# Scaling the last expert's tiles on ScalarE in every batch, with the order of the instructions written anew

## What is computed

```python
xn = layernorm(x)                                  # no scale or shift
q, k, v = xn @ Wq.T, xn @ Wk.T, xn @ Wv.T
attn = (q @ k.T) * tril(ones)                      # masked scores are 0, not minus infinity
attn = softmax(attn / sqrt(512)) @ v
gates = softmax(xn @ Wg); keep the top 2, divide by their sum
ffn = sum over experts e of gate[e] * (xn @ We[e] + be[e])
out = x + attn + ffn
```

## Time and profile before

| what | value |
|---|---|
| three runs, us | 120.26, 120.28, 120.30 (median 120.28) |
| profiled execution | 120.22 us, of which the span (first to last instruction) is 118.5 us |
| TensorE clock granted | full in the whole span |
| busy share of the span | TensorE 95%, VectorE 90%, ScalarE 84%, GpSimd 77% |

### The profile page before, as it was taken

How to read it: one execution, slowest core, us unless ns; L and a number is a source line. 1 busy time by engine, 2 the same in 40 slices (tenths; PEclk the granted TensorE clock), 3 DMA queues, 4 the chain that set the end, 5 groups by cost and what they waited for, 6 DMA issues and landing times.

```text
span 118.5 us, 2933 instructions
## 1 busy us (share of the span) xinstructions
PE 112.7 (95%) x733; PEld 103.5 (87%) x733; DVE 106.4 (90%) x532; ACT 99.0 (84%) x338; POOL 91.3 (77%) x183
## 2 busy tenths in 40 slices
PE   4986999999999999999999999999999999999990
PEld 4965879998999989998899989999899989899990
DVE  0689999989999899999999899999999898998892
ACT  2456899899897999899997989899997989978930
POOL 7349569899768996699768995799868995896970
PEclk9999999999999999999999999999999999999999
DMA  3759500000300011000300020000300030000033
GB/s 95 255 165 304 157 3 6 0 3 3 89 0 3 0 55 39 0 0 3 94 3 0 0 68 20 6 0 3 94 0 0 0 90 4 0 3 0 6 91 89
DMA packets 9233, 5.18 MB, mean 44 GB/s; under 512 B 384, under 2 KB 9088, under 8 KB 9216
## 3 DMA queue, kind: packets, MB, share of 16 engines
q1 hardware_dynamic: 8656, 4.66, 13.6%
q10 hardware_dynamic: 560, 0.33, 1.0%
HBM read 2.89 MB, written 2.10 MB: 42 GB/s over the span
## 4 chain that ended last, share of the span: by engine, by line
PE 87%; DMA 4%; ACT 3%; DVE 2%; SPq 1%; issue 1%; DVEq 0%
PE ring L248 15%; PE ring L252 14%; PE ring L249 14%; PE attb L306 13%; PE score L293 8%; PE score L252 4%; PE score L249 4%; PE score L248 4%; DMA w_f<-in_w_stacked_dram 4%; PE ring L324 3%; PE ring L345 2%; PE attb L358 1%; PE ring L335 1%; PE ring L337 1%; PE ring L334 1%; ACT c_s L906 1%
## 5 line engine op out<-in xcount | busy, mean ns | idle before, releaser
L922 ACT ACTIVATE ysc<-ring,gate 128x128 f32<-128x128 f32 x124 | 35.6, 388 | 0.8 <-PE ring L252 0.6
L248 PE MATMUL ring<-w_hi,xT_hi 128*128 128x512 f32 (+2 forms) x96 | 35.5, 370 | 0.4 <-ACT xT_hi L1001 0.4
L249 PE MATMUL ring<-w_lo,xT_hi 128*128 128x512 f32 (+2 forms) x96 | 32.5, 339 | 0.0
L252 PE MATMUL ring<-w_hi,xT_lo 128*128 128x512 f32 (+2 forms) x96 | 32.5, 338 | 0.0
L1130 POOL TENSOR_TENSOR ysc<-ysc,mix 128x256 f32<-128x256 f32 x31 | 22.9, 738 | 6.2 <-DVE mix L576 3.6
L1127 POOL TENSOR_TENSOR ysc<-ysc 128x256 f32<-128x256 f32 x31 | 22.8, 736 | 6.0 <-ACT ysc L922 6.0
L576 DVE SCALAR_TENSOR_TENSOR mix<-ring,gate,mix 128x128 f32<-128x128 f32 x65 | 22.4, 347 | 0.9 <-PE ring L252 0.3
L306 PE MATMUL attb<-c_s,probT 128*128 128x128 f32 x152 | 21.8, 274 | 0.0
L306 PEld LDWEIGHTS attb<-c_s,probT 128*128 128x128 f32 x152 | 20.1, 191 | 0.2
L248 PEld LDWEIGHTS ring<-w_hi,xT_hi 128*128 128x128 f32 x96 | 18.1, 189 | 2.1 <-ACT xT_hi L1001 0.6
L252 PEld LDWEIGHTS ring<-w_hi,xT_lo 128*128 128x128 f32 x96 | 18.1, 188 | 1.5 <-DVE xT_lo L509 0.2
(11 more groups left out here) (115 smaller groups left out, 237.8 us busy)
## 6 DMA issues: line engine op xcount, KB each, us to landing
x_all<-in_x_dram SPq DMA_DIRECT2D x7, 256.0 KB, 3.9
out_dram<-o_s SPq DMA_DIRECT2D x7, 256.0 KB, 2.3
w_f<-in_w_stacked_dram SPq DMA_DIRECT2D x1, 256.0 KB, 4.5
w_f<-in_w_stacked_dram SPq DMA_DIRECT2D x1, 192.0 KB, 4.4
w_f<-in_w_stacked_dram SPq DMA_DIRECT2D x1, 132.0 KB, 3.7
x_all<-in_x_dram ACTq DMA_DIRECT2D x1, 128.0 KB, 2.7
x_all<-in_x_dram SPq DMA_DIRECT2D x1, 128.0 KB, 2.5
wqk_s<-in_w_attention_dram ACTq DMA_DIRECT2D x1, 128.0 KB, 3.9
```

The lines of the kernel that those rows point to most:

```text
L248: nc.tensor.matmul(dst, hi, w_h, start=True, stop=False)
L249: nc.tensor.matmul(dst, hi, w_l, start=False, stop=False)
L252: return nc.tensor.matmul(dst, lo, w_h, start=False, stop=True)
L922: last = nc.scalar.mul(ysc[:, t, e, :], bank(f"A{t}", b)[:, e * P:(e + 1) * P], gate[:, b % 2, t, e:e + 1])
```

## The change

- ScalarE scales the last expert's product in every batch, four instructions of 128x128 (three in the last batch), behind `scale_experts(n, 0)`. `scale_last` and GpSimd's calls of it are gone.
- mix has five places per tile. B's results go to 0, 1 and 3 (`MIX_AT`), the scaled last expert to 2 in even and to 4 in odd batches, and GpSimd adds the pair 2:4 or 3:5. ScalarE therefore waits for the sums of two batches before, not of the one before.
- The order is written anew on all four engines, in the start, the loop and the end, and the ring's lists with it. In the start ScalarE makes w_hi of B first and of A later, GpSimd takes the bias split first, then w_lo of B, then of A; VectorE does the statistics of batch 1 before the second half of x_lo; TensorE takes the value sums behind two score tiles; ScalarE copies x of batch 1 before the first probabilities.

The diff, with eight columns of indentation taken off and the end's lists on TensorE and VectorE cut:

```diff
--- before.py
+++ after.py
@@ -52,12 +52,14 @@
 Y_AT, G_AT = P, 2 * P
 
 
-FIRST_GROUPS = """C0@0 C1@0 U@0 C2@0 C3@0 SV@0 B0@0 A0@0 X@1 A1@0 B1@0 U@1 C0@1 A2@0 C1@1 C2@1""".split()
-GROUPS = "B2- C3 A3- B3- SV DT- B0 A0 X+ A1 B1 U+ C0+ C1+ A2 C2+".split()
-LAST_GROUPS = """B2@-2 C3@-1 A3@-2 B3@-2 A0@-1 B0@-1 DT@-2 B1@-1 B2@-1 A1@-1 A2@-1 B3@-1 SV@-1 DT@-1 A3@-1""".split()
+FIRST_GROUPS = """C0@0 C1@0 U@0 C2@0 C3@0 SV@0 A0@0 X@1 B0@0 C0@1 A1@0 B1@0 U@1 A2@0 C1@1 C2@1""".split()
+GROUPS = "B2- C3 A3- B3- SV DT- B0 A0 X+ A1 C0+ B1 U+ C1+ A2 C2+".split()
+LAST_GROUPS = """B2@-2 C3@-1 A3@-2 B3@-2 A0@-1 B0@-1 DT@-2 B1@-1 B2@-1 A1@-1 SV@-1 B3@-1 A2@-1 A3@-1 DT@-1""".split()
 
 ROWS = 32
 G_ROW = 3
+
+MIX_AT = (0, 1, 3)
 
 
 class Chain:
@@ -136,7 +138,7 @@
 gsum, grec = (sb(n, [P, NT]) for n in ("gsum", "grec"))
 
 ysc = sb("ysc", [P, NT, 4, P])
-mix = sb("mix", [P, NT, 4, P])
+mix = sb("mix", [P, NT, 5, P])
 ffn = sb("ffn", [P, 2, NT, P])
 
 lhs_rows = sb("lhs_rows", [P, NT * ROWS], F32R)
@@ -396,24 +398,24 @@
     project_u(0)
     wide(0, "C", 2)
     wide(0, "C", 3)
-    value_sums(0)
     scores(0, 0)
     scores(0, 1)
-    wide(0, "B", 0)
+    value_sums(0)
+    wide(0, "A", 0)
     scores(0, 2)
-    wide(0, "A", 0)
     transpose_x(1)
     transpose_probs(0, 0)
+    wide(0, "B", 0)
+    scores(0, 3)
+    wide(1, "C", 0)
     wide(0, "A", 1)
-    transpose_probs(0, 1)
-    scores(0, 3)
     wide(0, "B", 1)
     project_u(1)
-    wide(1, "C", 0)
     wide(0, "A", 2)
-    attend(0, 0)
     wide(1, "C", 1)
     wide(1, "C", 2)
+    attend(0, 0)
+    transpose_probs(0, 1)
 
     for n in range(1, B - 1):
         wide(n - 1, "B", 2)
@@ -422,60 +424,60 @@
         scores(n, 0)
         transpose_probs(n - 1, 2)
         wide(n - 1, "A", 3)
+        wide(n - 1, "B", 3)
         transpose_probs(n - 1, 3)
-        wide(n - 1, "B", 3)
-        attend(n - 1, 2)
         value_sums(n)
         scores(n, 1)
+        attend(n - 1, 2)
         transpose_rows(n - 1)
         attend(n - 1, 3)
         bias(n - 1)
+        transpose_probs(n, 0)
         wide(n, "B", 0)
         wide(n, "A", 0)
         scores(n, 2)
-        transpose_probs(n, 0)
         transpose_x(n + 1)
         wide(n, "A", 1)
+        scores(n, 3)
+        transpose_probs(n, 1)
+        wide(n + 1, "C", 0)
         wide(n, "B", 1)
-        scores(n, 3)
         project_u(n + 1)
-        wide(n + 1, "C", 0)
         attend(n, 0)
-        transpose_probs(n, 1)
         wide(n + 1, "C", 1)
         wide(n, "A", 2)
         wide(n + 1, "C", 2)
 
...
@@ -572,8 +574,8 @@
         if i == 0 and with_y7:
 
             dve.wait_ge(S["x7_ready"], 1)
-        before = mix[:, t, i - 1, :] if i else mix[:, t, 3, :] if with_y7 else tile_ap(b, t)
-        ins = nc.vector.scalar_tensor_tensor(mix[:, t, i, :], bank(f"B{t}", b)[:, i * P:(i + 1) * P],
+        before = mix[:, t, i - 1, :] if i else mix[:, t, 4, :] if with_y7 else tile_ap(b, t)
+        ins = nc.vector.scalar_tensor_tensor(mix[:, t, MIX_AT[i], :], bank(f"B{t}", b)[:, i * P:(i + 1) * P],
                                              gate[:, b % 2, t, 4 + i:5 + i], before, ALU.mult, ALU.add)
         if i < 2:
             cnt["mix", b, t, i] = chain.mark(ins)
@@ -590,7 +592,7 @@
             chain.need(cnt["mix_a", e - 1])
         ins = nc.vector.scalar_tensor_tensor(
             mix[:, t, e % 2, :], bank(f"A{t}", b)[:, e * P:(e + 1) * P], gate[:, b % 2, t, e:e + 1],
-            mix[:, t, 2 if e == 0 else 1 - e % 2, :], ALU.mult, ALU.add)
+            mix[:, t, MIX_AT[2] if e == 0 else 1 - e % 2, :], ALU.mult, ALU.add)
         if e < 3:
             cnt["mix_a", e] = chain.mark(ins)
         else:
@@ -740,143 +742,143 @@
     a_low(0)
     x_lo_half(0, 0)
     first_sums(0)
-    x_lo_half(0, 1)
     normal_stats(1, 0)
-    token_sums_pairs(0)
     normal_stats(1, 1)
     normal_stats(1, 2)
     normal_stats(1, 3)
+    x_lo_half(0, 1)
+    token_sums_pairs(0)
     normal_finish(1)
     token_sums_later(0)
     u_lo(0)
     gate_max(0)
+    mask_scores(0, 0)
     gate_drop(0)
-    mask_scores(0, 0)
+    gate_below(0)
     mask_scores(0, 1)
-    gate_below(0)
     negate_max(0, 0)
+    gate_sum(0)
     negate_max(0, 1)
+    gate_rec(0)
     sv_rows(0, 0)
+    gate_out(0)
     sv_rows(0, 1)
-    gate_sum(0)
     sv_rows(0, 2)
-    gate_rec(0)
-    gate_out(0)
+    x_lo(1)
     mix_b(0, 0, 0)
+    token_sums(1)
     mix_b(0, 0, 1)
     mix_b(0, 0, 2)
-    x_lo(1)
-    token_sums(1)
 
     for n in range(1, B - 1):
+        mask_scores(n - 1, 2)
         mix_b(n - 1, 1, 0)
-        mask_scores(n - 1, 2)
         mix_b(n - 1, 1, 1)
         negate_max(n - 1, 2)
         mix_b(n - 1, 1, 2)
         u_lo(n)
         normal_stats(n + 1, 0)
         normal_stats(n + 1, 1)
-        normal_stats(n + 1, 2)
         mask_scores(n - 1, 3)
         mix_b(n - 1, 2, 0)
+        negate_max(n - 1, 3)
         mix_b(n - 1, 2, 1)
-        negate_max(n - 1, 3)
+        normal_stats(n + 1, 2)
         mix_b(n - 1, 2, 2)
+        token_sums_pairs(n)
+        mask_scores(n, 0)
         gate_max(n)
         normal_stats(n + 1, 3)
+        softmax_sum(n - 1)
+        token_sums_later(n)
+        softmax_tot(n - 1)
         gate_drop(n)
-        softmax_sum(n - 1)
-        token_sums_pairs(n)
-        softmax_tot(n - 1)
-        token_sums_later(n)
+        normal_finish(n + 1)
         gate_below(n)
-        normal_finish(n + 1)
+        negate_max(n, 0)
+        mask_scores(n, 1)
+        softmax_rec(n - 1)
+        negate_max(n, 1)
         mix_b(n - 1, 3, 0)
-        mask_scores(n, 0)
+        gate_sum(n)
         mix_b(n - 1, 3, 1)
-        gate_sum(n)
-        negate_max(n, 0)
+        gate_rec(n)
         mix_b(n - 1, 3, 2)
-        gate_rec(n)
-        softmax_rec(n - 1)
         gate_out(n)
-        mask_scores(n, 1)
         sv_rows(n, 0)
         sv_rows(n, 1)
+        sv_rows(n, 2)
         mix_b(n, 0, 0)
-        sv_rows(n, 2)
+        finish_tile(n - 1, 0)
+        finish_tile(n - 1, 1)
         mix_b(n, 0, 1)
-        finish_tile(n - 1, 0)
+        finish_tile(n - 1, 2)
         mix_b(n, 0, 2)
-        finish_tile(n - 1, 1)
-        negate_max(n, 1)
-        finish_tile(n - 1, 2)
-        finish_tile(n - 1, 3)
         x_lo(n + 1)
         token_sums(n + 1)
-
+        finish_tile(n - 1, 3)
+
...
+    sv_rows(B - 1, 0)
+    softmax_rec(B - 1)
+    sv_rows(B - 1, 1)
+    mix_b(B - 1, 3, 0)
     finish_tile(B - 2, 2)
-    mix_b(B - 1, 3, 0)
+    mix_b(B - 1, 3, 1)
     finish_tile(B - 2, 3)
-    mix_b(B - 1, 3, 1)
+    sv_rows(B - 1, 2)
     mix_b(B - 1, 3, 2)
-    sv_rows(B - 1, 0)
-    sv_rows(B - 1, 1)
-    softmax_rec(B - 1)
     mix_a(0)
-    sv_rows(B - 1, 2)
     mix_a(1)
     mix_a(2)
     finish_tile(B - 1, 0)
+    mix_a(3)
     finish_tile(B - 1, 1)
-    mix_a(3)
     finish_tile(B - 1, 2)
     finish_last(B - 1)
 
@@ -925,9 +927,11 @@
     def scale_last_act(b):
 
         act.wait_ge(S["gate_ready"], b + 1)
-        act.wait_ge(S["ffn_ready"], b * NT)
-        for t in range(NT - 1):
-            last = nc.scalar.mul(mix[:, t, 3, :], c_s[:, b % 2, t, Y_AT:Y_AT + P], gate[:, b % 2, t, 7:8])
+        if b > 1:
+
+            act.wait_ge(S["ffn_ready"], (b - 1) * NT)
+        for t in range(NT if b < B - 1 else NT - 1):
+            last = nc.scalar.mul(mix[:, t, 2 + 2 * (b % 2), :], c_s[:, b % 2, t, Y_AT:Y_AT + P], gate[:, b % 2, t, 7:8])
         last.then_inc(S["y7_ready"], 1)
 
     def softmax_exp(b, t):
@@ -1009,30 +1013,31 @@
     act.wait_ge(S["w_c"], 16)
     nc.scalar.copy(w_hi[:, c_cols], w_f[:, c_cols]).then_inc(S["wc_ready"], 1)
 
+    wb_high(0)
     a_high(0)
-    wa_high(0)
     x_hi_half(0, 0)
     x_hi_half(0, 1)
+    wa_high(0)
     c_copy(0, 0)
-    wb_high(0)
     c_copy(0, 1)
     u_hi(0)
     c_copy(0, 2)
     c_copy(0, 3)
-    sv_high(0)
     normalize(1)
     gate_exp(0)
+    sv_high(0)
     softmax_exp(0, 0)
     softmax_exp(0, 1)
+    x_hi(1)
     probs_copy(0, 0)
-    x_hi(1)
     scale_experts(0, 0)
+    scale_last_act(0)
+    c_copy(1, 0)
     scale_experts(0, 1)
     u_hi(1)
-    c_copy(1, 0)
+    scale_experts(0, 2)
     masked_exp(0)
     probs_copy(0, 1)
-    scale_experts(0, 2)
     softmax_exp(0, 2)
     c_copy(1, 1)
     c_copy(1, 2)
@@ -1041,23 +1046,24 @@
     for n in range(1, B - 1):
         softmax_exp(n - 1, 3)
         probs_copy(n - 1, 2)
+        scale_experts(n - 1, 3)
         probs_copy(n - 1, 3)
-        gate_exp(n)
-        scale_experts(n - 1, 3)
-        rows_copy(n - 1)
         sv_high(n)
         softmax_exp(n, 0)
+        gate_exp(n)
+        rows_copy(n - 1)
+        softmax_exp(n, 1)
         normalize(n + 1)
+        probs_copy(n, 0)
         scale_experts(n, 0)
         x_hi(n + 1)
-        probs_copy(n, 0)
-        softmax_exp(n, 1)
+        scale_last_act(n)
         scale_experts(n, 1)
+        c_copy(n + 1, 0)
         u_hi(n + 1)
-        c_copy(n + 1, 0)
         probs_copy(n, 1)
+        c_copy(n + 1, 1)
         softmax_exp(n, 2)
-        c_copy(n + 1, 1)
```

(74 more changed lines are left out.)

18 lines of the change are left out of this document (8 added, 10 removed).

## The result

The changed kernel takes 121.85 us (median of four runs, 121.71 to 121.86) against 120.27 for the kernel before beside it: 1.0129 times as long, interval 1.0113 to 1.0145, so 1.58 us slower. The profiled run took 121.86 us, its span is 120.1.

What follows compares the result with a forecast made beforehand. TensorE was taken as the bound from the middle of the first batch to the end. 120.22 + 0.9 (start) + 0.1 (middle) + 0 (end) = 121.2 us; own range 120.9 to 121.5, whole range 119.9 to 122.1.

Steps and rivals of the forecast that it cites:

- the mechanism named for the start: Start: a chain from GpSimd's run through the held pair sum and normalize to the loop's first B2, +0.9 us.
- ScalarE becomes the bound: Rival, middle batches: ScalarE busy 13.39 us in 13.24, 0.15 us x 7 on top, 122.2 us; 13%.
- Step 1, GpSimd's run: Start: GpSimd's run, beginning with the bias split, lasts from 7.1 to 10.6, 0.5 us won.
- Step 2, statistics ahead of xT_lo: Start: VectorE's batch 1 statistics go first; pair sum at 9.5 to 9.9, TensorE waits for xT_lo some 0.8 us.
- Step 3, the hold: Start: VectorE's pair sum is held until GpSimd's w_lo of A ends, at 10.65; bounds 0.15 or 1.1 us.
- The pair sum isn't held: Rival, start: pair sum slips through, normalize at 12.05, B2 at 20.45, +0.3, about 120.6 us; 17%.
- the second rival's: Start, on the hold: without the rule on two SBUF inputs, the sum would be that of the rival called second.
- Steps 4 to 6: Start: normalize at 12.65, score tile 3 at 16.15, then 4.9 us to B2 at 21.05 instead of 20.13, +0.9 us.
- Middle, ScalarE: Middle batches: four added scalings, 1.16 us, fit in 1.57 us of room; cost nothing, upper end 0.15 us a batch.
- Middle, U's bank: Middle batches: B2 waits for uT_lo, a 1.8 us chain; 0 to 0.05 us a batch, taken as 0.1 for six.
- End: End: VectorE's five instructions behind bias_early keep their order; A3's move gives room before them only: 0.
- GpSimd: Middle batches: loses its scaling, has 2.4 us slack; its second addition for tile 0 waits for ScalarE's scalings: nothing.

Runs made afterwards that it cites:

- run 11: Kernel before, with GpSimd's bias split first in the start and the pair sum reading one operand through an overlapping window: 120.06 us, 0.9989.
- run 8: Changed kernel with the pair sum written as a reduction over an overlapping window of one operand instead of adding two: 121.38 us, 1.0095.
- run 6: Changed kernel with the start's order of before on all engines and batch 0's scaling on GpSimd: 120.80 us, 1.0056.
- Run 12: The kernel of run 8, with ScalarE also copying the first probabilities ahead of x of batch 1: 121.35 us, 1.0097.
- run 5: Changed kernel with all its orders, but the scaling of batches 0 to 6 back on GpSimd: 122.01 us, 1.0156.
- run 9: Changed kernel's start and end, with the loop's order of before and the scaling on GpSimd: 122.50 us, 1.0197.
- Run 4: Changed kernel with the end's order of before on all engines: 121.59 us, 1.0104.
- run 7: Old order, batch 0's scaling on GpSimd, ScalarE's scalings of batches 1 to 6 in two pairs, behind scale_experts(n, 1) and masked_exp(n): 153.69 us.

## Why the prediction came out as it did

The forecast was +0.9, +0.1 and 0 for start, middle and end. By the trace it was +1.02, +0.19 and +0.33, together 1.54 of the 1.58 us measured; the runs give back 0.95 to 1.05 for the start and 0.15 to 0.26 for the end. The direction and the mechanism named for the start were right, and it decided. The size was not: the sum is 0.6 us short, and 121.85 us lies above the forecast's own range of 120.9 to 121.5. It lies in the whole range only because that was drawn up to 122.1 for the case that ScalarE becomes the bound, which didn't happen; that part is luck. All three terms erred to the same side, the end by most.

- *Step 1, GpSimd's run.* Forecast 7.1 to 10.6, measured 7.35 to 10.86. It began 0.25 us later because the first tiles were ready at 7.28, not 7.03. That isn't the change's: run 11, with the order of before, has the first power of GpSimd at 1.20 us and the first tiles from 6.08, against 5.92 in the earlier trace rows. The last section says what goes with it.
- *Step 2, statistics ahead of xT_lo.* The pair sum started at 9.89, in the range of 9.5 to 9.9, and TensorE's waits for xT_lo and uT_lo are the 0.58 and 0.53 above.
- *Step 3, the hold.* Right: 0.99 us until GpSimd's w_lo ended, and run 8 takes it away with the form of the instruction. The rival *The pair sum isn't held* is out. Its price is smaller than the prediction had it: 0.37 to 0.47 measured, while forecast and rival are 0.6 apart. The rival's own chain came true in run 8: veps is held in the pair sum's place, but GpSimd is through only then (10.86) and starts rstd 0.11 later, from where normalize follows 1.34 us later as forecast. The working leaned on weak rows: the 0.75 us was another kind of instruction, as the rival says, while four holds of this very sum stood in the same trace (run 8), and by them the rival deserved less than its 17%. The sentence on "the second rival's" sum means this rival, which is the first.
- *Steps 4 to 6.* Normalize at 12.79 (forecast 12.65), score tile 3 at 16.20 (16.15), from there to B2 4.87 us (4.9), B2 at 21.07 (21.05). The rest of the start's loss, 1.05 - 0.47 = 0.58 us, lies behind normalize: runs 8 and 6 start it within 0.08 us of each other (12.31, 12.23), and from there to B2 are 8.29 us in the one and 7.72 in the other. That is the new order there; which engine's list does it was not separated. Run 12 shows that it isn't one wait that could be lifted.
- *Middle, ScalarE.* Costed at nothing, and nothing it is: run 5. The condition written beside it, that the new order must put the scalings where ScalarE waits, was the important half: in the old order they cost 1.1 us a batch in one place and 0.65 in another. The rival *ScalarE becomes the bound* fails for this kernel, but with 13.14 of 13.26 us busy not by much.
- *Middle, U's bank.* The chain of 1.8 us was 1.74 (59.09 to 60.83), and the wait came. The size was off: 0 to 0.05 a batch, taken as 0.1 in all, was 0.03 each, 0.19 in all. Runs 5 and 9 put it on the order: 13.27 with the changed groups, 13.23 with the old, GpSimd scaling in both, and B2's pair at 0.21 to 0.22 us in run 5 and at 0.17 to 0.18 in run 9. Single batches scatter by as much: run 11, with the old order, has three of 13.26 to 13.27 without this wait, and two of 13.23.
- *End.* This is the term that failed: "that gives room before the five only: 0". It looked at VectorE's last five instructions and not at what comes before them. VectorE's last two finishes of batch 6 now stand behind the first value-sum rows and among the mixes of tile 3 of batch 7, and TensorE's attend needs the bank that the last of them empties. Of the 0.33 us this wait is 0.16. Run 4 gives 0.18 us back by its trace, 0.15 to 0.26 by its time.
- *GpSimd.* Costed at nothing for its wait on ScalarE: right here (6.6 us of waiting in 7 times, and TensorE doesn't feel it), and in run 7, where it waited up to 6.7 us, TensorE's waits for the bias rows came to 20 us.

Open is which list costs the 0.58 us behind normalize, and whether run 5's 0.16 us is more than scatter. No more was tried on these.
